# A vision tower, a two-way Mamba layer and a mixture of experts: one VectorE reduction for the minima of both images

## What is computed

```
q, k, v = jnp.moveaxis(qkv, 2, 0)
attn = jnp.einsum('bthd,bshd->bhts', q, k) * scale
attn = jax.nn.softmax(attn, axis=-1)
out = jnp.einsum('bhts,bshd->bthd', attn, v).reshape(Bx, Tx, C)
```

## Time and profile before

| what | value |
|---|---|
| median of 3 runs | 8892.51 us (8873.36 to 8898.86) |
| the profiled execution's own time | 8887.31 us |
| its span, first to last instruction | 8885.5 us |
| mean granted TensorE clock | 0.925 of full speed |
| busy PE / DVE / ACT / POOL | 7020.2 / 7053.6 / 6179.2 / 806.7 us |
| reductions of scores (L768) | 2048, 1087.7 us busy, mean 562 ns |

### The profile page before, as it was taken

The page is one execution under the profiler, slowest core; times in us unless marked ns, Lnnn a source line. Parts: engine busy times, 40 slices in busy tenths (PEclk is TensorE's granted clock), DMA queues, the critical chain, the costliest instruction groups (busy, mean ns, idle before and its releaser), DMA issues. The chain is left out here.

```text
span 8885.5 us, 117469 instructions
## 1 busy us (share of the span) xinstructions
PE 7020.2 (79%) x33290; PEld 3894.5 (44%) x33290; DVE 7053.6 (79%) x9195; ACT 6179.2 (70%) x13424; POOL 806.7 (9%) x554
## 2 busy tenths in 40 slices
PE   6777777788888888888888888888888888888561
PEld 3444444444444444444444444444444444444330
DVE  2788888888888888888888888888888888888743
ACT  4766666677777777777777777777777777777434
POOL 0133333400000000000000000000000000000055
PEclk8988989899999999999999999999999999999775
DMA  2233333233333323333333333333333333332356
GB/s 91 105 119 119 109 109 108 92 118 117 115 120 117 118 107 123 114 119 114 115 117 115 114 115 121 113 112 115 121 117 109 122 115 117 111 122 109 127 116 199
DMA packets 282498, 1034.03 MB, mean 116 GB/s; under 512 B 37570, under 2 KB 129526, under 8 KB 273824
## 3 DMA queue, kind: packets, MB, share of 16 engines
q1 hardware_dynamic: 248352, 1009.77, 31.6%
q0 software_dynamic: 33792, 21.18, 1.5%
HBM read 951.57 MB, written 90.94 MB: 117 GB/s over the span
## 5 line engine op out<-in xcount | busy, mean ns | idle before, releaser
L1047 PE MATMUL psS<-KM,Q 128*99 128x394 f32 x4096 | 1718.4, 536 | 351.2 <-ACT PTs L578 260.8
L843 DVE TENSOR_TENSOR_SCAN hs<-dA,hs 128x1576 f32<-128x1576 f32 x512 | 1762.3, 3442 | 63.0
L572 ACT ACTIVATE P<-psS,least_s 99x197 f32<-99x197 f32 x4096 | 1413.4, 431 | 469.4 <-DVE least_s L768 466.3
L1054 PE MATMUL psS<-cst,P 99*99 99x99 f32 x8192 | 1047.9, 268 | 345.1 <-ACT P L572 300.6
L1054 PEld LDWEIGHTS psS<-cst,P 99*99 99x99 f32 x8192 | 912.2, 176 | 895.9 <-ACT P L572 654.5
L768 DVE TENSOR_REDUCE least_s<-psS 99x2 f32<-99x394 f32 x2048 | 1087.7, 562 | 261.7 <-PE psS L1047 229.6
L649 ACT ACTIVATE dA<-dt_,aneg 128x394 f32<-128x394 f32 x2048 | 1184.4, 621 | 28.9 <-DVE hs L843 18.9
L578 ACT ACTIVATE PTs<-psS 99x396 f32<-99x396 f32 x2048 | 985.9, 517 | 223.6 <-PE psS L1054 219.0
L1047 PEld LDWEIGHTS psS<-KM,Q 128*99 128x99 f32 x4096 | 626.4, 174 | 1086.9 <-ACT PTs L578 578.0
L829 DVE TENSOR_TENSOR hs<-hs,u 128x1576 f32<-128x1576 f32 x512 | 917.6, 1792 | 42.2 <-DMA hs<-bc_scratch 40.7
L1139 PE MATMUL psY<-hs,cst 128*128 128x394 f32 x2048 | 831.4, 536 | 116.1 <-DVE hs L852 115.7
(11 more groups left out here) (214 smaller groups left out, 9499.9 us busy)
## 6 DMA issues: line engine op xcount, KB each, us to landing
hs<-bc_scratch SPq DMA_DIRECT2D x512, 788.0 KB
cr<-bc_scratch SPq DMA_DIRECT2D x512, 788.0 KB
pat<-patches SPq DMA_DIRECT2D x64, 1176.0 KB, 5.9
more_scratch<-zeros SPq DMA_DIRECT2D x64, 197.0 KB, 5.2
rows_scratch<-hs SPq DMA_DIRECT2D x1, 12352.0 KB, 43.1
PTs<-more_scratch SPq DMA_DIRECT2D x24, 512.0 KB
sum_scratch<-HW SPq DMA_DIRECT2D x64, 148.5 KB
hs<-rows_scratch SPq DMA_DIRECT2D x24, 386.0 KB
```

What stands on the lines that cost most here:

```text
L572: last = nc.scalar.activation(P[:, r, b, m, 0:T], psS[0:CT, 2 * r + b, m * T:(m + 1) * T], ACT.Exp, bias=least_s[:, r, b, m:m + 1], scale= ...
L843: nc.vector.tensor_tensor_scan(h, a, h, 0.0, ALU.mult, ALU.add).then_inc(scan_ready, 1)
L1047: mm(psS[0:CT, 2 * r + b, 0:2 * T].rearrange("p (e t) -> p e t", e=2), Q[:, r, b, q * CT:(q + 1) * CT], KM[:, r, h % 2 * 2:h % 2 * 2 + 2, ...
L1054: last = nc.tensor.transpose(psS[0:CT, 2 * r + b, at:at + CT], P[:, r, b, m, k * CT:(k + 1) * CT], c("ident")[0:CT, 0:CT])
```

## The change

DVE's `scores` does nothing for image 0; for image 1 it waits for both scores (`round_done` counts both) and takes all four minima in one `tensor_reduce` over the two neighbouring banks psS[2r] and psS[2r + 1], 788 elements into 4. `max_done` goes up once a round in place of twice, and ACT's `scores` of either image waits for that one count. There are 16 reductions a step. No other instruction is added, removed or altered.

```diff
             def scores(i, r, n, b):
-                act.wait_ge(max_done[r], i * ROUNDS * 2 + n * 2 + b + 1)
+                act.wait_ge(max_done[r], i * ROUNDS + n + 1)
...
             def scores(i, r, n, b):
-                dve.wait_ge(round_done[r], i * ROUNDS * 4 + n * 4 + b + 1)
-                nc.vector.tensor_reduce(least_s[:, r, b, :], psS[0:CT, 2 * r + b, 0:2 * T].rearrange("p (e t) -> p e t", e=2), axis=AX, op=ALU.min).then_inc(max_done[r], 1)
+                if b:
+                    dve.wait_ge(round_done[r], i * ROUNDS * 4 + n * 4 + 2)
+                    nc.vector.tensor_reduce(least_s[:, r, :, :], psS[0:CT, 2 * r:2 * r + 2, 0:2 * T].rearrange("p b (e t) -> p b e t", e=2), axis=AX, op=ALU.min).then_inc(max_done[r], 1)
```

The tables `STAGES` and `PLACE` are replaced as a whole. What an engine then goes through is shown here for one step as the two tables give it (units with a star, those of the pair before with a minus; `score101` is score, role 1, round 0, image 1). DVE before, then after, up to the end of the rounds:

```
-*-scan4 *-input5 norm10 *-output4 *sigmoid0 conv0 *-scan5 norm00 *-half4 score100 *gate0 score101 *-input6 score000 *-output5 score001 score110 score111 *-scan6 *-half5 *-input7 score010 score011 score120 *dt0 score121 *-output6 score020 score021 *-scan7 *-half6 *-output7 score130 score030 score031 score131 *-half7 *input0 *scan0 *-ys1 *-merge score140 score141 score040 score041 *input1 *output0 *-route score150 score050 score051 score151 *scan1 *half0 *input2 score160 score161 *output1 score060 score061 *sigmoid1 *scan2 *half1 score170 score070 score071 score171 *gate1 *input3 *output2 *scan3 *half2 *dt1
+*-scan4 *-input5 norm10 *-output4 *sigmoid0 conv0 *-scan5 norm00 score101 *-half4 *gate0 *-input6 score001 *-output5 score111 *-scan6 *-half5 *-input7 score011 score121 *dt0 *-output6 score021 *-scan7 *-half6 *-output7 score131 *-half7 score031 *input0 *scan0 *-ys1 *-merge score141 score041 *input1 *output0 *-route score151 score051 *scan1 *half0 *input2 score161 *output1 score061 *sigmoid1 *scan2 *half1 score171 score071 *gate1 *input3 *output2 *scan3 *half2 *dt1
```

DVE from there to the end of the step:

```
-den1 den0 wo1 wo0 norm11 norm01 *output3 gate1 *half3 gate0 sig1 sig0 up1 up0 down1 *ys0 *input4 down0 norm12
+den1 den0 wo1 wo0 norm11 norm01 *output3 gate1 *half3 gate0 sig1 *ys0 sig0 up1 up0 down1 *input4 norm12 down0
```

PE, rounds 0 and 1 and round 5, and the end of the step:

```
-conv0 qkv1 norm00 score100 qkv0 score101 turn100 *xproj0 score000 turn101 score001 score110 score111 *-sum4 turn110 turn000 turn111 turn001
+conv0 qkv1 norm00 score100 score101 qkv0 *-sum4 turn100 turn101 *xproj0 score000 score001 score110 turn000 score111 *dtproj0 turn110 turn001 turn111
...
-turn140 turn040 turn141 *-leave *-route turn041 score150 score050 score051 score151 *project1.0 turn150 turn151 turn050 turn051
+turn140 turn141 turn040 turn041 score150 score151 score050 score051 *-route *project1.0 turn050 turn150 turn151 turn051
...
-*sum1 turn171 *xproj1 turn070 turn071 value11 *dtproj1 value01 den1 den0 wo1 wo0 norm11 norm01 gate1 gate0 *sum2 *sum3 up1 up0 down1 down0 norm12
+*xproj1 turn171 turn070 turn071 value11 *dtproj1 value01 den1 den0 *sum1 wo1 wo0 norm11 norm01 gate1 gate0 *sum2 *sum3 up1 up0 down1 norm12 down0
```

ACT, rounds 0 and 1, and the end of the step:

```
-*gate0 *-decay7.0 score100 qkv0 keys00 score101 keys11 turn100 score000 turn101 *-decay7.1 *xproj0 score001 score110 score111 turn110 keys01 turn000
+*gate0 *-decay7.0 score100 score101 qkv0 keys00 keys11 turn100 turn101 *-decay7.1 score000 score001 *xproj0 keys01 score110 turn000 score111 turn110
...
-den1 den0 *decay4.0 squar11 squar01 norm11 norm01 gate1 gate0 sig1 sig0 *decay4.1 *decay4.2 *decay4.3 *decay5.0 *decay5.1 *decay5.2 squar12 *decay5.3 norm12
+den1 den0 squar11 *decay4.0 squar01 norm11 norm01 *decay4.1 gate1 gate0 sig1 sig0 *decay4.2 *decay4.3 *decay5.0 squar12 norm12 *decay5.1 *decay5.2 *decay5.3
```

More of the change, by code:

```diff
@@ L82, in role_stages @@
     return out
-STAGES = [('square', 1, 0), ('norm', 1, 0), ('conv', 0), ('square', 0, 0), ('qkv', 1), ('keys', 1, 0), ('norm', 0, 0), ('score', 1, 0, 0), ('qkv', 0), ('keys', 0, 0), ('score', 1, 0, 1), ('keys', 1, 1), ('turn', 1, 0, 0), ('score', 0, 0, 0), ('turn', 1, 0, 1), ('score', 0, 0, 1), ('score', 1, 1, 0), ('score', 1, 1, 1), ('turn', 1, 1, 0), ('keys', 0, 1), ('turn', 0, 0, 0), ('turn', 1, 1, 1), ('turn', 0, 0, 1), ('score', 0, 1, 0), ('score', 0, 1, 1), ('score', 1, 2, 0), ('turn', 0, 1, 0), ('score', 1, 2, 1), ('turn', 0, 1, 1), ('score', 0, 2, 0), ('score', 0, 2, 1), ('keys', 1, 2), ('turn', 1, 2, 0), ('turn', 1, 2, 1), ('keys', 0, 2), ('turn', 0, 2, 0), ('turn', 0, 2, 1), ('score', 1, 3, 0), ('score', 0, 3, 0), ('score', 0, 3, 1), ('keys', 0, 3), ('score', 1, 3, 1), ('turn', 0, 3, 0), ('turn', 0, 3, 1), ('keys', 1, 3), ('turn', 1, 3, 0), ('turn', 1, 3, 1), ('value', 0, 0), ('value', 1, 0), ('score', 1, 4, 0), ('score', 1, 4, 1), ('score', 0, 4, 0), ('score', 0, 4, 1), ('turn', 1, 4, 0), ('turn', 0, 4, 0), ('turn', 1, 4, 1), ('turn', 0, 4, 1), ('score', 1, 5, 0), ('score', 0, 5, 0), ('score', 0, 5, 1), ('score', 1, 5, 1), ('turn', 1, 5, 0), ('turn', 1, 5, 1), ('turn', 0, 5, 0), ('turn', 0, 5, 1), ('score', 1, 6, 0), ('score', 1, 6, 1), ('score', 0, 6, 0), ('score', 0, 6, 1), ('turn', 1, 6, 0), ('turn', 1, 6, 1), ('turn', 0, 6, 0), ('turn', 0, 6, 1), ('score', 1, 7, 0), ('score', 0, 7, 0), ('score', 0, 7, 1), ('score', 1, 7, 1), ('turn', 1, 7, 0), ('turn', 1, 7, 1), ('turn', 0, 7, 0), ('turn', 0, 7, 1), ('value', 1, 1), ('value', 0, 1), ('den', 1), ('den', 0), ('wo', 1), ('wo', 0), ('square', 1, 1), ('square', 0, 1), ('norm', 1, 1), ('norm', 0, 1), ('gate', 1), ('gate', 0), ('sig', 1), ('sig', 0), ('up', 1), ('up', 0), ('down', 1), ('down', 0), ('square', 1, 2), ('norm', 1, 2)]
@@ new lines @@
+STAGES = [('square', 1, 0), ('norm', 1, 0), ('conv', 0), ('square', 0, 0), ('qkv', 1), ('keys', 1, 0), ('norm', 0, 0), ('score', 1, 0, 0), ('score', 1, 0, 1), ('qkv', 0), ('keys', 0, 0), ('keys', 1, 1), ('turn', 1, 0, 0), ('turn', 1, 0, 1), ('score', 0, 0, 0), ('score', 0, 0, 1), ('keys', 0, 1), ('score', 1, 1, 0), ('turn', 0, 0, 0), ('score', 1, 1, 1), ('turn', 1, 1, 0), ('turn', 0, 0, 1), ('turn', 1, 1, 1), ('score', 0, 1, 0), ('score', 0, 1, 1), ('score', 1, 2, 0), ('score', 1, 2, 1), ('turn', 0, 1, 0), ('turn', 0, 1, 1), ('keys', 1, 2), ('turn', 1, 2, 0), ('score', 0, 2, 0), ('score', 0, 2, 1), ('turn', 1, 2, 1), ('keys', 0, 2), ('turn', 0, 2, 0), ('turn', 0, 2, 1), ('score', 1, 3, 0), ('score', 1, 3, 1), ('score', 0, 3, 0), ('score', 0, 3, 1), ('keys', 0, 3), ('turn', 0, 3, 0), ('turn', 0, 3, 1), ('keys', 1, 3), ('turn', 1, 3, 0), ('turn', 1, 3, 1), ('value', 0, 0), ('value', 1, 0), ('score', 1, 4, 0), ('score', 1, 4, 1), ('score', 0, 4, 0), ('score', 0, 4, 1), ('turn', 1, 4, 0), ('turn', 1, 4, 1), ('turn', 0, 4, 0), ('turn', 0, 4, 1), ('score', 1, 5, 0), ('score', 1, 5, 1), ('score', 0, 5, 0), ('score', 0, 5, 1), ('turn', 0, 5, 0), ('turn', 1, 5, 0), ('turn', 1, 5, 1), ('turn', 0, 5, 1), ('score', 1, 6, 0), ('score', 1, 6, 1), ('score', 0, 6, 0), ('score', 0, 6, 1), ('turn', 1, 6, 0), ('turn', 1, 6, 1), ('turn', 0, 6, 0), ('turn', 0, 6, 1), ('score', 1, 7, 0), ('score', 1, 7, 1), ('score', 0, 7, 0), ('score', 0, 7, 1), ('turn', 1, 7, 0), ('turn', 1, 7, 1), ('turn', 0, 7, 0), ('turn', 0, 7, 1), ('value', 1, 1), ('value', 0, 1), ('den', 1), ('den', 0), ('wo', 1), ('square', 1, 1), ('wo', 0), ('square', 0, 1), ('norm', 1, 1), ('norm', 0, 1), ('gate', 1), ('gate', 0), ('sig', 1), ('sig', 0), ('up', 1), ('up', 0), ('down', 1), ('square', 1, 2), ('norm', 1, 2), ('down', 0)]
```

2 lines of the change are left out of this document (1 added, 1 removed).

## The result

Over four runs the kernel with the change took 9006.42 us in the median (9000.19 to 9036.17), the kernel before on the same chip 8884.59 us. The ratio is 1.0147 with a 95% interval of 1.0121 to 1.0173, so it is slower by 1.5%, outside the range that was forecast and on the other side of no change. The profiled execution took 9036.17 us (span 9034.3) and is the longest of the four; its mean granted TensorE clock was 0.900, where that of the other three was 0.904 to 0.907 and that of the profiled execution before 0.925. So the time at the lower clock that is read from this trace is somewhat high for the kernel: (0.905 - 0.900) x 2 x 9034 / 61 is about 1.5 us a step above a median run, by estimate.

What follows compares the result with a forecast made beforehand. Rounds were taken as set by DVE's queue plus its waits, the stretch between by a chain of small hops through three engines. Terms summed to -1.65 us a step, -100 us over 61 steps: 8787 us, range 8695 to 8905.

Steps and rivals of the forecast that it cites:

- rival 1: TensorE's clock: one slow stretch goes, 8683 us (chance 0.12), or another appears, 8891 (0.20 together with second scores eating the gain).
- reductions: DVE's queue: 16 merged reductions of 0.973 us replace 32, saving 2.1 us a step (ends 1.0 and 2.8).
- waits for scores: DVE's merged reductions wait for both images' scores: 3.6 us against 2.8, +0.8 us a step (ends 0 and +3.6).
- wait for the load: Next quarter's input lands no earlier, so DVE time saved before it becomes wait: +0.6 us a step (0 to +1.2).
- The end of a step: PE's norm (1,2) goes ahead of down (0), so H and project come earlier: -0.65 and -0.3 us a step.
- Rival 3: Lockstep: merged reductions waiting for second scores hold up DVE's queue and ACT's decays; 8957 us, chance of slower 0.18.
- Rival 2: Second-score waits come to +2.4 us, eating nearly all the gain; chance 0.20 together with an added clock stretch.
- theory A: Explanation set up after the result: minima come together, exponentials and PE's transposes start late, PE stands longer, lower clock follows.

Runs made afterwards that it cites:

- the nine fillers: Nine unneeded matmuls a step ahead of PE's waits, added to the kernel with the change (8874.67 us) and to separate reductions in the new tables (8724.05 us).
- split_shared_wait: New tables with two separate reductions in place of the merged one, ACT's exponentials of either image waiting for both minima: 9027.57 us, ratio 1.0171.
- split_filled: Separate reductions in the new tables, plus nine unneeded matmuls a step ahead of PE's waits: 8724.05 us, ratio 0.983.

## Why the prediction was wrong

**What failed.** The forecast was faster by 1.1%; it is 1.5% slower. Two steps failed together: the sum has no term for ACT's wait when the first image's exponentials are held for the second image's minima, and it leaves the time at the lower clock as it was. The larger of the two is the clock, rival 1. I had the earlier trace rows in hand, three slow stretches of 3.4 us a step, and priced the clock as one such stretch more or less, so "if another appears elsewhere, the gain falls to nothing: 8891". What came is 9.5 us more a step, nearly three such stretches (19.7 against 10.2), 9.5 x 0.37 = 3.5 us; in a median run it is some 8 us by the estimate above. I asked where one gap would go away and where one might open, and never what the change as a whole does to the clock. By place in the step, from the clock record of 40 steps (us a step at the lower level):

| us after the step's start | before | new tables, separate reductions | with the change |
|---|---|---|---|
| 0 to 24 | 1.9 | 0.0 | 0.6 |
| 24 to 44 | 0.7 | 5.9 | 7.4 |
| 44 to 88 | 2.7 | 0.0 | 0.1 |
| 88 to 100 | 0.0 | 0.5 | 2.7 |
| 100 to 116 | 4.4 | 3.4 | 4.2 |
| 116 to the end | 0.5 | 0.5 | 4.7 |
| sum | 10.2 | 10.3 | 19.7 |

Rival 1's own guess came true: the stretch ahead of which down (0) now stands, at some 68 us, is gone, and so is the one at 8 us. But the tables brought as much at 24 to 44 us, and the merged reduction with its wait added 9.4 us, most of it from 88 us on.

**Why I didn't ask.** The sum holds the waits of DVE and nothing else of the chain. That ACT's exponentials of image 0 now wait for the minima of image 1 stands in my text as a fact, with no price. I took the reduction of DVE's queue as the limit and the consumer's start as covered by it. The measured price: at about equal low time (6.8 us) the new tables take 123.16 us a step with separate reductions (15 steps) and 123.94 with the merged one (8 steps), 0.8 us for the merging and its late start alone; under the nine fillers at 3.4 us it is 123.47 against 124.63, 1.2 us. The rest of the 4.4 us between 124.4 and 128.85 is the clock: 9.4 us more of it, times 0.37, is 3.5 us.

**The terms of the sum.**

| term, us a step | forecast | measured |
|---|---|---|
| reductions | -2.1, busy time 14.9 | busy time 16.97 to 15.35, -1.6 |
| waits for scores | +0.8, to 3.6 | 2.83 to 3.97, +1.1 |
| wait for the load | +0.6, to 1.2 | 0.55 to 1.49, +0.9 |
| the step at low time 6.8 | -1.65 | 124.81 to 123.94, -0.9 |
| time at the lower clock | as before | 10.2 to 19.7, worth +3.5 |
| a step | 124.6 | 128.7 |

*The reductions* came out as worked: 973 ns alone, and a queued pair of merged ones in 1.86 (below). The total is about 0.5 us short of the forecast: 583.3 / 608 = 0.959 us each lies near the 0.973 of one that was waited for, not halfway to the 0.884 of one that was queued. And I credited the merging with it; the separate reductions in the new tables are at 16.3 us a step already (40 steady steps). Of the 1.6 us, some 0.7 are the tables' and 1.0 the merging's.

*The waits for scores* were right in size and place: at the first round of role 0 the merged reduction waits 2.42 us where I said 2.2, and *the load* 1.54 where I said 1.2. But their sum hides two parts. With separate reductions in the new tables the waits for scores are 75.5 / 40 = 1.9 us a step, less than before, and those for the load 1.1 already. So merging by itself adds 2.1 us of waits for scores and saves 1.0 of busy time: it costs DVE 1.1 us a step, and only together with the tables does it look near the forecast. In split_shared_wait DVE waits only 98.8 / 40 = 2.5 us, and the kernel is as slow, so it is not DVE's own balance that decides. Rows of DVE's timeline after, which answer to the earlier trace rows:

```profile
4982.36 1.86 DVE L769 TENSOR_REDUCE least_s<-psS 99x4 f32<-99x788 f32 x2
...
5149.83 0.57 DVE L798 TENSOR_TENSOR X<-X,psS 128x394 f32<-128x394 f32 x1 [1.20 <-PE psS L1099]
...
5153.27 0.63 DVE L764 SCALAR_TENSOR_TENSOR H<-X,vec,rs 128x394 f32<-128x394 f32 x1 [1.16 <-ACT rs L554]
...
5174.93 0.98 DVE L769 TENSOR_REDUCE least_s<-psS 99x4 f32<-99x788 f32 x1 [2.42 <-PE psS L1048]
...
5203.22 1.80 DVE L830 TENSOR_TENSOR hs<-hs,u 128x1576 f32<-128x1576 f32 x1 [1.54 <-DMA hs<-bc_scratch]
```

*The end of a step:* from down 1's add to H it was 5072.70 - 5068.76 = 3.94 us and is 5153.27 - 5149.83 = 3.44 us, 0.5 shorter where I forecast 0.65. This, like the rest of what pays, is the tables'.

**The rivals.** Rival 1 was the right mechanism with the wrong size, and its worst case stopped at no change. Rival 3, which carried my chance of slower, had the right sign: that one image now waits for the other is what costs. But it looked for the cost in DVE's queue, and the score waits rose by 1.1 us and not by 3.6, far from the 2.45 us from which it decides; that is what the merged reduction does in the old tables. Here the cost comes by ACT's start and the clock. Rival 2 had the row that mattered, ACT's 6.5 us a step of waiting for minima, and read it as a reason that shortening DVE's queue pays. The same row says that anything that makes a first minimum later is paid at once: it is 10.1 us now.

**What stays open.** Which of the gaps, alone or together, brings the lower clock is not settled: the same 1.91 us gap was followed by both levels. The filling matmuls lower the waits of PE and raise its work at once, so they show that the clock is the cause of most of the loss, not what the chip measures. The one line of ACT in split_shared_wait shows that the late first exponential brings the low time, from 10.3 to 21.3 us a step. That it does so by longer gaps of PE, as theory A has it, is not shown. PE's idle time is 21.0 us a step before, 18.7 with separate reductions, 18.5 with the shared wait and 19.5 with the change, so it doesn't rise with the low time (though work at the lower clock fills part of what would be idle). And from 12 to 28 us, right ahead of the long low stretch and at full clock in all three kernels, PE is idle for 3.5 us with separate reductions, where the stretch came in 13 of 40 steps, 2.9 with the shared wait, where it came in 33, and 3.0 with the change, where it came in 23.

## What to carry to other kernels

Price a merged instruction by the start of its first consumer, not only by the engine that it relieves: here 1 us a step of VectorE's time was saved, and the first image's whole chain waited for the second. Where TensorE shares a step with slower engines, take the granted clock of every step from the trace and compare kernels at equal clock before blaming an order or an instruction; where it runs low behind gaps, try a few matmuls of no use in front of them, which here were worth 62 us net with nine a step and 105 with six on the better order (8785.74 to 8680.83), and 132 us on the worse. And test the tables and the instruction apart, since a change that comes with both can hide a gain of 0.9% under a loss of 2.4%.

## What the runs showed of the hardware

TensorE's clock can stay low through a stretch in which it is busy without a pause: 13.60 us of 13.60 at a granted 0.50, behind a gap of 1.91 us, while the same stretch of another step, behind the same gap, ran at 1.00. The same 32 products took 2.87 and 1.55 us. The Trainium skill (TensorE: Matmul & The Clock Gate, Part 1) says that throttled is the default and activity releases it; the trace agrees that work added ahead of gaps raised the clock (0.900 to 0.936 over the whole kernel with nine fillers a step), and the 13.6 us above show PE busy without a pause and still at the lower level.

A low stretch that was cured in one place came back in part in another. Taking sum 1 back removed 5.5 us a step at 28 us and 2.8 came back elsewhere; two matmuls ahead of turn (1,7,0) removed 7.4 and 3.3 came back. The order of the work in those other places was the same. Nor does low time cost the same everywhere: 0.37 us of step a us in the kernel with the change, and 0.04 us for 3.4 us of it in split_filled (123.47 against 123.43).

Instructions in VectorE's queue overlap by about 0.09 us for the longer reduction too: two merged ones in a row took 1.86 us, where one alone takes 0.973.
